# Second layer norm of a transformer block: the scale applied to the token rows, division and shift inside TensorE's turns, five Gelu buffers

## What is computed

```
ada = timestep_embed @ ada_w + ada_b          # one row of 6*256 for each sequence
shift1, scale1, gate1, shift2, scale2, gate2 = split(ada, 6)
x1 = _ln(x) * (1 + scale1) + shift1
... 16 heads of attention on x1, projected by out_w ...
x  = x + gate1 * attn_out
x2 = _ln(x) * (1 + scale2) + shift2           # _ln: (x - mean) / sqrt(var + 1e-6) over 256 features
h  = gelu(x2 @ ffn_w1 + ffn_b1)               # 256 -> 1024
x  = x + gate2 * (h @ ffn_w2 + ffn_b2)        # 1024 -> 256
```

## Time and profile before

| | us |
|---|---|
| median of 3 runs | 516.11 (515.8 to 516.94) |
| profiled execution, device time | 515.61 |
| its span, first to last instruction | 513.8 |
| TensorE busy | 449.6 (88%) |
| DVE busy | 434.9 (85%) |
| ACT busy | 316.3 (62%) |
| mean granted clock | 0.97 of full speed |

### The profile page before, as it was taken

The page is one execution under the profiler, slowest core; times in us unless marked ns, Lnnn a source line. Parts: engine busy times, 40 slices in busy tenths (PEclk is TensorE's granted clock), DMA queues, the critical chain, the costliest instruction groups (busy, mean ns, idle before and its releaser), DMA issues.

```text
span 513.8 us, 13730 instructions
## 1 busy us (share of the span) xinstructions
PE 449.6 (88%) x4980; PEld 307.5 (60%) x4980; DVE 434.9 (85%) x1705; ACT 316.3 (62%) x880; POOL 48.6 (9%) x77
## 2 busy tenths in 40 slices
PE   2999989998999899997498997689888888888887
PEld 2655665567556665575244443667676766766666
DVE  4969786787777876889988786999999999999994
ACT  1387855786487748786458755465655646555563
POOL 3010330224021211123000000000000000000000
PEclk9999999999999999999789999698989999999999
DMA  8972402200202000000000000000000000000000
GB/s 294 417 311 63 106 7 76 61 21 0 82 21 62 0 0 1 0 1 0 0 1 1 0 1 0 3 3 0 1 1 11 11 1 10 1 11 11 1 10 22
DMA packets 10127, 20.82 MB, mean 41 GB/s; under 512 B 1456, under 2 KB 4720, under 8 KB 9456
## 3 DMA queue, kind: packets, MB, share of 16 engines
q1 hardware_dynamic: 9536, 19.89, 11.2%
q10 hardware_dynamic: 560, 0.60, 0.3%
HBM read 19.40 MB, written 1.08 MB: 40 GB/s over the span
## 4 chain that ended last, share of the span: by engine, by line
DVE 42%; PE 40%; ACT 6%; issue 5%; POOL 4%; DMA 1%; ACTq 0%; DVEq 0%
PE bank L804 34%; DVE base L1649 5%; DVE lin L1751 5%; POOL ptx L477 4%; DVE qs L1655 4%; DVE cub L1643 3%; PE score L804 3%; DVE sq L1637 3%; DVE pacc L1761 3%; PE spare L804 2%; ACT ao_sb L541 2%; DVE thlo L1633 1%; DMA vec<-vecs 1%; DVE qn L1655 1%; DVE acc L1421 1%
## 5 line engine op out<-in xcount | busy, mean ns | idle before, releaser
L804 PE MATMUL bank<-x,pairs_store 128*128 128x512 f16 x384 | 85.6, 379 | 0.0
L804 PE MATMUL score<-th,coup_part 128*128 128x32 f16 x1024 | 47.2, 179 | 18.1 <-ACT th L788 17.2
L804 PEld LDWEIGHTS bank<-x,pairs_store 128*128 128x128 f16 x384 | 37.1, 98 | 42.8 <-DVE x L1219 0.4
L477 POOL TENSOR_TENSOR ptx<-pt,ptx 32x256 f16<-32x256 f32 x64 | 44.7, 699 | 189.4 <-ACT ptx L573 185.8
L541 ACT ACTIVATE big<-bank,pass_b 128x512 f16<-128x512 f32 x64 | 42.1, 684 | 24.3 <-DVE pass_b L1347 14.4
L788 ACT ACTIVATE th<-qs 128x64 f16<-128x64 f32 x96 | 24.5, 255 | 47.5 <-DVE qs L1655 47.5
L804 PEld LDWEIGHTS score<-th,coup_part 128*128 128x128 f16 x1024 | 34.7, 97 | 31.1 <-ACT th L788 29.7
L1359 DVE SCALAR_TENSOR_TENSOR big<-bank,pass_b,big 128x512 f16<-128x512 f32 x64 | 45.7, 742 | 8.0 <-ACT big L541 7.3
L804 PE MATMUL bank<-pairs_store,ao_sb 128*128 128x256 f16 x384 | 46.6, 273 | 4.7 <-DVE acc L1421 1.4
L804 PEld LDWEIGHTS bank<-pairs_store,ao_sb 128*128 128x128 f16 x384 | 35.5, 97 | 13.6 <-issue 3.6
L804 PE MATMUL bank<-pairs_store,x 128*128 128x512 f16 x192 | 43.4, 379 | 0.0
(11 more groups left out here) (210 smaller groups left out, 1041.8 us busy)
## 6 DMA issues: line engine op xcount, KB each, us to landing
wqk_sb<-wqk SPq DMA_DIRECT2D x16, 256.0 KB, 3.0
wv_sb<-wv SPq DMA_DIRECT2D x4, 512.0 KB, 5.6
wo_sb<-wo SPq DMA_DIRECT2D x4, 512.0 KB, 4.2
f_sb<-ffn_w SPq DMA_DIRECT2D x2, 1024.0 KB, 14.2
ao_sb<-xtok SPq DMA_DIRECT2D x4, 256.0 KB, 6.1
big<-ada_w SPq DMA_DIRECT2D x1, 1024.0 KB, 9.7
x_sb<-xT SPq DMA_DIRECT2D x1, 1024.0 KB, 13.3
w_sb<-w1T SPq DMA_DIRECT2D x1, 1024.0 KB, 16.4
```

What stands on the lines that cost most here:

```text
L477: nc.gpsimd.tensor_tensor(ptx[s, 1, :, s], pt[s], ptx[s, 0, :, s], ALU.subtract).then_inc(ptx_ready, 1)
L804: return nc.tensor.matmul(dst, lhsT, rhs, start=start, stop=stop, **kw)
```

## The change

In words:

- **Rows at the start.** `shift2` and `scale2` are made as rows of a sequence (`mod_rows`, 32x512, in the second bank of `score`), copied out by ACT, given bias and the 1 by DVE in `late_start`. `scale_rows` goes to memory, and after the scores of head 14 (the third head of the last pass) SP loads it back as `scale_tok`, eight transfers of 128 KB in which each row is repeated for its 32 tokens.
- **The scale on the token side.** `scale_x2(g)` on DVE writes (x - mean) * scale for a group. The division is done by TensorE: ACT writes `root_diag`, a diagonal matrix of one over the root (`diagonals`), and the turn is a float32 product with that matrix in place of the unit matrix. The shift is a product too, of `shift_rows` with a repeated unit matrix, summed in the same bank.
- **High and low parts from PSUM.** `turned_high(h)` on ACT and `x1_low(h)` on DVE read `score`. `normalise_x2` and `modulate` are gone.
- **Orders.** On TensorE the turns of the second half stand inside `output_layer(0)`, before block 4, and no longer before it. On DVE `last_heads(2)` stands behind `x1_low(0)`, and the low parts of Gelu blocks are spread over the work on the second half. Five Gelu buffers. The banks of `hidden_layer(0)` are dealt anew.
- **Products that nobody reads** (`unread`): 8 before and 6 behind the first turns, 20 behind the last gates.

```diff
+        scale_tok = big[:, 0:2048].rearrange("p (m h d) -> p m h d", m=G // 2, h=2)
...
+        gelu_of = (npos[:], za[:], var[:, 1], rstd[:, 0], rstd[:, 1])
...
-        USE_F1 = [AFTER + KB, AFTER + 3 * KB + MB]
+        USE_F1 = [[AFTER + n for n in (2, 5, 6, 7, 3, 4, 8, 9)], [AFTER + 3 * KB + MB + m for m in range(MB)]]
...
+            sp.wait_ge(rows_stored, 16)
+            sp.wait_ge(scores_ready, (NQUAD - 1) * QUAD + 3)
+            for h in range(NH):
+                for b in range(NB4):
+                    sp.dma_start(scale_tok[b * T:(b + 1) * T, :, h],
...
+            def diagonals(h):
 
                 act.wait_ge(tok_scale_ready, h + 1)
+                if h:
+                    act.wait_ge(x2_turned, h)
                 for g in range(h * G // 2, (h + 1) * G // 2):
-                    nc.scalar.activation(x2_norm[:, g], acc[:, g], ACT.Identity, bias=tok_shift[:, g:g + 1],
-                                         scale=tok_rstd[:, g:g + 1]).then_inc(x2_normed, 1)
+                    nc.scalar.activation(root_diag[:, g % (G // 2)], ident32[:], ACT.Identity, scale=tok_rstd[:, g:g + 1]
+                                         ).then_inc(diag_ready, 1)
+
+            def turned_high(h):
+
+                s = slice(h * HALF, (h + 1) * HALF)
+                act.wait_ge(x2_turned, h + 1)
+                for k in range(KB):
+                    nc.scalar.activation(x1_pair[:, 0, k, s], score[:, k], ACT.Copy).then_inc(x1_high_ready, 1)
...
-            ada_chunks(spare[:, D:], 3 * KB, 6 * KB).then_inc(ada2_summed, 1)
+            ada_chunks(spare[:, D:], 5 * KB, 6 * KB)
+            for k in range(KB):
+                last = mm(score[0:B, 1], cond_sb[:, k], adaw_sb[:, k, 3 * D:5 * D], k == 0, k == KB - 1)
+            last.then_inc(ada2_summed, 1)
...
+            def turn_scaled(h):
+
+                pe.wait_ge(rows_ready, 2)
                 if h:
-                    pe.wait_ge(turned_read, KB * h)
+                    pe.wait_ge(x1_ready, NH + h)
+                nb = B // NH
+                for k in range(KB):
+                    mm(score[:, k].rearrange("p (b t) -> p b t", t=T), shift_rows[:, k * P:(k + 1) * P],
+                       ident32[:, h * nb:(h + 1) * nb].unsqueeze(2).broadcast_to([P, nb, T]), True, False, skip_group_check=True)
                 for g in range(h * G // 2, (h + 1) * G // 2):
-                    pe.wait_ge(x2_normed, g + 1)
+                    pe.wait_ge(x2_scaled, g + 1)
+                    pe.wait_ge(diag_ready, g + 1)
                     for k in range(KB):
-                        last = nc.tensor.transpose(score[:, k, g % 4 * P:(g % 4 + 1) * P], x2_norm[:, g, k * P:(k + 1) * P],
-                                                   ident32[:])
+                        last = mm(score[:, k, g % 4 * P:(g % 4 + 1) * P], x2_norm[:, g, k * P:(k + 1) * P],
+                                  root_diag[:, g % (G // 2)], False, g % 4 == 3, skip_group_check=True)
                 last.then_inc(x2_turned, 1)
 
+            def unread(dst, count):
+
+                for _ in range(count):
+                    mm(dst, scaled_eye[:], ptx[:, 0, 0:G // 2].rearrange("p g n -> p (g n)"), True, True)
+
+            pe.wait_ge(eye_ready, 1)
             turn_x2(0)
-            turn_normed(0)
+            unread(spare[:], 8)
+            turn_scaled(0)
+            unread(spare[:], 6)
...
+                    if (h, m, ob) == (0, MB // 2, 0):
+                        turn_scaled(1)
+                        turn_x2(1)
...
             hidden_layer(0)
-            turn_normed(1)
-            turn_x2(1)
             output_layer(0)
...
             last_gates()
+            unread(score[:, 1], 20)
...
+                V.tensor_tensor(mod_rows, mod_rows, mod_bias, ALU.add).then_inc(rows_ready, 1)
...
+            def scale_x2(g):
+
+                if g % (G // 2) == 0:
+                    dve.wait_ge(scale_loaded, 16 * NH * NB4)
+                    dve.wait_ge(tok_var_ready, 1 + g + G // 2)
+                V.scalar_tensor_tensor(x2_norm[:, g], acc[:, g], tok_mv[:, g, 0:1], scale_tok[:, g % (G // 2), g // (G // 2)],
+                                       ALU.subtract, ALU.mult).then_inc(x2_scaled, 1)
```

More of the change, by code:

```diff
@@ L1482, in _, with hidden_low @@
                     add_heads(0, 3)
-                    token_scale(0)
+                    half_var(0)
+                    for g in range(G // 2):
+                        scale_x2(g)
+                    dve.wait_ge(tok_std_ready, 2)
+                    ln.step(V.reciprocal(tok_rstd[:, 0:G // 2], tok_std[:, 0:G // 2]))
+                    root_step(0, 0)
+                    root_step(0, 1)
+                    root_step(0, 2, done=True)
                     close_heads(2)
-                    last_heads(2)
                 assert own.n == STEPS and pairs[0] == PAIRS
             own.n, own.base = start + NQUAD * STEPS, 0
-            dve.wait_ge(ada2_ready, 6)
-            modulate(0)
+            dve.wait_ge(ada2_ready, 5)
             x1_low(0)
             mlp_lows(5, 6)
+            last_heads(2)
+            def hidden_low(h, m):
+                n = h * MB + m
+                hi, lo = (hid_pair[:, m, c, h * HALF:(h + 1) * HALF] for c in range(2))
+                dve.wait_ge(hid_high_ready, n + 1)
+                V.tensor_tensor(lo, gelu_of[n % NGELU], hi, ALU.subtract).then_inc(hid_low_ready, 1)
+            hidden_low(0, 0)
             close_heads(3)
@@ L1494, in _ @@
             token_var(1)
-            dve.wait_ge(xT_loaded, 16)
-            token_scale(1)
-            def hidden_lows(h):
-                for m in range(MB):
-                    n = h * MB + m
-                    if n == 2:
-                        mlp_lows(7)
-                    if n == MB - 1:
-                        modulate(1)
-                    if MB + 2 <= n < MB + 6:
-                        mlp_lows(n + 2)
-                    hi, lo = (hid_pair[:, m, c, h * HALF:(h + 1) * HALF] for c in range(2))
-                    dve.wait_ge(hid_high_ready, n + 1)
-                    V.tensor_tensor(lo, gelu_of[n % 2], hi, ALU.subtract).then_inc(hid_low_ready, 1)
-                if h == 0:
-                    x1_low(1)
+            hidden_low(0, 1)
+            half_var(1)
+            scale_x2(4)
+            root_seed(0)
+            scale_x2(5)
+            root_seed(1)
+            hidden_low(0, 2)
+            root_seed(2)
+            scale_x2(6)
+            root_step(1, 0)
+            scale_x2(7)
+            root_step(1, 1)
+            root_step(1, 2)
+            root_step(1, 0)
+            root_step(1, 1)
+            hidden_low(0, 3)
+            root_step(1, 2)
+            root_step(1, 0)
+            root_step(1, 1)
+            root_step(1, 2, done=True)
+            dve.wait_ge(xT_loaded, 16)
             def wait_full(use):
@@ L1578, in _ @@
             own.wait()
-            hidden_lows(0)
+            hidden_low(0, 4)
+            hidden_low(0, 5)
+            mlp_lows(7)
+            hidden_low(0, 6)
+            x1_low(1)
+            hidden_low(0, 7)
             dve.wait_ge(late_loaded, 9 * 16)
@@ L1593, in _ @@
             residual(0)
-            hidden_lows(1)
+            for m in range(MB):
+                if 2 <= m < 6:
+                    mlp_lows(m + MB + 2)
+                hidden_low(1, m)
             dve.wait_ge(hid_low_ready, NH * MB)
```

138 lines of the change are left out of this document (78 added, 60 removed).

## The result

The changed kernel takes 522.06 us in the median of 4 runs (521.61 to 523.95), the kernel before beside it 515.95 us (515.54 to 516.94). The ratio is 1.0122 with a 95% interval of 1.0094 to 1.0151: slower by 6.1 us. Forecast were 520.8 us in a range of 517.6 to 523.0, and slower with a chance of 0.83. The profiled execution of the changed kernel is its longest, 523.95 us (span 522.1); the spans of the others are 519.8 to 520.3.

What follows compares the result with a forecast made beforehand. TensorE is never idle from 273.20 to the last gates, so an earlier output_layer(0) or work added behind it reaches the end. 0.35 - 2.3 + 4.6 + 2.2 - 0.15 = +4.7 us: median 520.8, range 517.6 to 523.0.

Steps and rivals of the forecast that it cites:

- start: Rows of shift and scale: TensorE saves net 0.25 us, DVE additions in late_start cost 0.6; sum +0.35 us.
- start of the output layer: output_layer(0) in the first half starts at 270.9 instead of 273.20, -2.3 us, after TensorE stands still 4.9 us.
- turns inside it: Second half's shifts (1.71), division (1.95) and turn_x2(1) (0.95) inside output_layer(0), in a stretch without a hole: +4.6 us.
- clock behind the hole: TensorE's clock falls in the 4.9 us hole before output_layer(0): +2.2 us, bounds 0 and 4.5.
- recurrence: First steps 0.1 to 0.3 us shorter if the 20 unread products keep the clock up: -0.15 us; step length unchanged.
- DVE's queue: Before output_layer(0): 15.4 us of DVE instructions from 255.45 end with mlp_lows(7) at 270.85 and set the layer's start.
- rival 2: DVE is not late before output_layer(0): 513.7 us; the change is faster if mlp_lows(7) ends before 268.4; chance 0.10.
- rival 1: The clock holds over the 4.9 us hole before output_layer(0), as at 272: +2.5 us, 518.6; chance 0.17.
- the 3 to 6 that I had named as its sign: In the 10 us after the hole before output_layer(0), the granted clock is 0.5 for 3 to 6 us.
- Unread products: Those around the first turns keep the clock at 2.4 GHz, so hidden_layer(0) takes 10.4 us instead of 12.68.
- rival 3: Unread products do not hold the clock; hidden_layer(0) ends 2.2 us later, hole only 2.8 us: 518.6 to 520.8; chance 0.06.
- Five buffers: Gelu buffers cost nothing and free ACT from DVE, but bring nothing behind 273.2, where TensorE was not waiting for ACT.

Runs made afterwards that it cites:

- e12: e8 with close_heads(3) and last_heads(3) also moved ahead of hidden_low(0, 0); 518.78 us, ratio to the kernel before 1.0047.
- e1: The changed kernel with mlp_lows(7) made right behind pieces 5 and 6 on DVE; 514.97 us, ratio to the kernel before 0.9977.
- e6: The changed kernel without the 20 unread products behind the last gates; 522.78 us, ratio to the kernel before 1.0142.
- e13: The changed kernel with the second half's shift left out, so part of the computation is missing; 520.92 us, ratio to the kernel before 1.0097.
- e7: The changed kernel with two Gelu buffers in place of five; 519.78 us, ratio to the kernel before 1.0073.
- e3: The changed kernel with the second half's turns ahead of output_layer(0) instead of inside it; 516.34 us, ratio to the kernel before 1.0006.
- e4: The changed kernel without the 8 and 6 unread products around the first half's turns; 521.42 us, ratio to the kernel before 1.0109.
- e8: The changed kernel with last_heads(2) moved ahead of x1_low(0) on DVE; 522.25 us, ratio to the kernel before 1.0111.
- e9: The changed kernel with the moves of e8 and e1 together; 514.24 us, ratio to the kernel before 0.9965.
- e11: The kernel before with 8 unread products behind its first turn_x2 and 20 behind its first turned half; 516.61 us against 515.88.
- e10: e1 with 31 unread products in place of 20 behind the last gates; 515.10 us, ratio to the kernel before 0.9983.

## Why the prediction was right

The forecast was right in sign and in the mechanism up to the recurrence, and 1.3 us short. By its own steps, in the profiled executions:

| step | forecast | measured | how |
|---|---|---|---|
| start | +0.35 | +0.20 | `turn_x2(0)` at 247.21, before 247.01 |
| start of the output layer | -2.3 | -2.33 | 271.07 - 273.20 - 0.20 |
| turns inside it | +4.6 | +4.38 | 283.60 - 279.22 |
| clock behind the hole | +2.2 | +2.97 | 8.15 - 5.18 |
| last gates to the recurrence | 0 | +0.03 | 5.25 - 5.22 |
| recurrence | -0.15 | +1.10 | 127 steps: 177.13, before 176.03 |
| after the last step | 0 | +1.95 | 14.62, before 12.67 |

The sum is 8.3 us, the difference of the two spans. The medians differ by 6.1, because the last row and the clock's are high in this execution.

*Start.* 20.61 against 20.92 is -0.31 (forecast -0.25). The wait behind `late_start` grew from 0.31 to 0.48 us, and one of 0.23 came ahead of it; at 52.30, before 52.10, +0.20 was left, and as much at `turn_x2(0)`.

*DVE's queue* was the step on which the sign hung, and it held: `mlp_lows(7)` ended at 271.01, forecast 270.85. e12 moved it and TensorE followed; e1 took it out and the change became faster than the kernel before. One sentence of rival 2 was wrong: it put the break-even at an end of 268.4. In e12 the piece ends at 268.63, which by that sentence costs 0.2 us; the kernel is 2.9 us slower than the kernel before. The clock, which I had left out there, falls behind its hole of 2.65 us too (6.87 - 5.18 = 1.7 us).

*The clock* fell, and the row at 272 of the kernel before, over a hole of 1.93 us, did not carry over (rival 1). It stayed down for 6.8 us, longer than the 3 to 6 that I had named as its sign. Its price is 3.0 us in this execution and 2.0 to 2.3 by e6, e13 and the medians, so my 2.2 was near, but by luck: I took it from the difference of two hidden layers, and the slow one began at 256.84, some 6.4 us after the clock fell at 250.4, and so met only the last part of a longer fall. The rule in the Trainium skill ("TensorE: Matmul & The Clock Gate", section "HAM oscillation — how this bites in real kernels"), idle holes between bursts bring half rate, agrees with the trace here (0.50 behind the hole of 4.95 us). Not every hole did it: behind those of e7, one of them 3.00 us, the clock stayed at 1.00.

*Turns.* The float32 division at 0.12 us a pass took 1.95 us, to the digit; the stretch is 0.2 shorter because the tail that I counted overlaps the next product. e13 shows the shifts' part, e3 the whole.

*Unread products.* They did hold the clock ahead of the hidden layer (rival 3 is out: e4 shows the layer at 12.21 us without them), and this was worth nothing, since the hole behind it took it. *Five buffers* were forecast at nothing; e7 shows that in this order they cost 2.3 us, through the clock. The 0.15 us that I gave the 20 products at the end did not come (e6).

*The recurrence* is the term that failed, and its 1.25 us (+1.10 where I had -0.15) are as much as the whole forecast was short. I took its step length as unchanged, and said that a changed one would make the prediction wrong; on the mean it is 0.6% longer. The typical step is 1.35 us in both, and the difference sits in a few steps: apart from the first (1.75 in both), the fourteenth takes 1.79 us (before 1.44), and six more take 1.59 to 1.77 (before, one: 1.77). In four of the seven DVE stands still with no releaser, in the steps 14, 48, 82 and 116; the kernel before has one such row in the same stretch, the last one here:

```profile
349.64 0.23 DVE L1740 SCALAR_TENSOR_TENSOR base<-cub,lin 128x64 f32<-128x64 f32 x1 [0.30 <-issue]
...
397.54 0.23 DVE L1746 SCALAR_TENSOR_TENSOR qn<-score,base 128x64 f32<-128x64 f32 x1 [0.27 <-issue]
...
444.56 0.23 DVE L1842 SCALAR_TENSOR_TENSOR lin<-qs,lin 128x64 f32<-128x64 f32 x1 [0.17 <-issue]
...
491.99 0.20 DVE L1820 TENSOR_SCALAR q_group<-qn 128x64 f32<-128x64 f32 x1 [0.21 <-issue]
```

```profile
485.54 0.22 DVE L1765 SCALAR_TENSOR_TENSOR pacc<-qs,pacc 128x64 f32<-128x64 f32 x1 [0.16 <-issue]
```

These waits are 0.95 us against 0.16, 0.79 us more, beside the 1.10 to be explained. The first of them stands in the same step of e1, 8 us earlier, so the time does not bring it; in e8, e9 and e12, whose DVE code is in another order, partly other steps are long (71 in place of 82). The traces show two things more. From one of these rows to the next it is 313, 314 and 313 DVE instructions (in e9, from its step 14 to its step 48, 313 as well), so the waits sit at fixed places of DVE's instruction list. And 0.66 to 0.90 us behind the start of each row a transfer of instructions starts (queue q14 of the page: 350.31, 398.44, 445.23, 492.65; before 486.21, 0.67 behind). Both point at the loading of DVE's code. That is argued and not shown, since no run moved the code and nothing else, and most of such transfers (12 in the recurrence of either kernel) have no wait ahead of them. The cause of step 105, 0.34 us longer than before with no such row, is open altogether.

*After the last step* the clock fell at the wrong moment: the 24 products of 128 columns took 2.72 us, before 1.50. The profiled executions of e8 and e12 have it too (14.53 and 14.59 us after the last step). The other spans of the change are some 2 us shorter, so its median does not hold it. In the traces of the other nine altered versions of the change this stretch takes 12.93 to 13.07 us, so some 0.35 us over the 12.67 of the kernel before are likely in the median; their cause was not looked into.

```profile
509.67 2.72 PE L838 MATMUL bank<-big,f_sb 128*128 128x128 f16 x24
```

## What to carry to other kernels

When a change makes one engine finish a stage sooner, write down the queue of the engine that it waits for next, instruction by instruction: here a single 0.6 us weight split, queued behind work with no hurry, made a hole of 4.95 us, and moving it turned +6.1 us into -1.2. Price a hole twice, once by its length and once by the clock behind it (2.0 to 3.0 us here), and as long as there is a hole, place work that waits for nothing else in it, not behind it. Here buffers and filler that sped up the stage ahead of the hole only lengthened the hole.

## What the runs showed of the hardware

- The length of a hole alone did not tell whether the clock falls: behind 1.97 us (the kernel before, at 250), 2.65 (e12), 3.26 (e4), 4.66 (e8) and 4.95 it fell, behind 1.36 (e3), 1.93 (the kernel before, at 273), 1.94 (e11) and 3.00 with 0.73 and 0.87 close behind (e7) it did not.
- The same hole ahead of the same work did not cost the same each time: behind 4.94 or 4.95 us the first half took 7.15 us (e6), 7.38 (e13) and 8.15 (the change), against 5.18 at full clock.
- In the recurrence the clock falls with hardly any wait ahead of it (0.22 us in e10), while TensorE is busy for 1.5 us or more of each stretch of 2 us by the profile (1.50 in 324 to 326, 1.55 in 325 to 327).
- DVE's waits of 0.16 to 0.30 us with no releaser sit at fixed places of its instruction list, 313 or 314 instructions apart in the change, not at fixed times.
